# A decoder layer with 39 expert tiles: fewer waits at each tile on TensorE, two barriers replaced by waits, four pieces of work in another order

## What is computed

```python
x = layernorm(x + attention(x, Wq, Wk, Wv, Wo, bo))     # causal, 16 heads of 64
x = layernorm(x + slot_attention(x, ctx, ...))          # 3 iterations with a GRU cell
x = layernorm(ffn(x, ...))

def ffn(x):                                             # 2048 tokens of 256
    values, experts = top_k(softmax(x @ gate_w + gate_b), k=2)
    values = values / (sum(values) + 1e-9)
    out_e  = gelu(x @ ew1[e] + eb1[e]) @ ew2[e] + eb2[e]   # 8 experts, 1024 wide
    return x + gelu(x @ sh_w1 + sh_b1) @ sh_w2 + sh_b2 + sum(values * out_of_the_two_experts)
```

## Time and profile before

| what | us |
|---|---|
| median of 3 runs | 873.48 (873.08 to 873.78) |
| the profiled execution | 875.04 |
| its span, first to last instruction | 873.8 |
| PE busy | 851.6 (97%) |
| DVE, ACT, POOL busy | 605.5, 547.6, 391.0 |

### The profile page before, as it was taken

One profiled execution on the slowest core, in us unless ns is written; L12 is line 12 of the kernel. 1 busy time (PEld: TensorE's weight loads), 2 busy tenths in 40 slices (PEclk: granted clock), 3 DMA queues, 4 the chain that ended last, 5 costly groups with the idle time before them and its releaser, 6 DMA issues. The chain is left out here.

```text
span 873.8 us, 22869 instructions
## 1 busy us (share of the span) xinstructions
PE 851.6 (97%) x8048; PEld 675.1 (77%) x8048; DVE 605.5 (69%) x1638; ACT 547.6 (63%) x1218; POOL 391.0 (45%) x494
## 2 busy tenths in 40 slices
PE   8999999999999999999999999998999999999996
PEld 7788888888888888767676666675788888887864
DVE  5676779775668685656666767888776666666655
ACT  5888887867676776565756565664444444444455
POOL 4544534352433475334544442544635445454443
PEclk9999999999999999999999999999999999999999
DMA  9843424334233321500000000299775555655426
GB/s 312 223 146 127 164 99 146 123 121 146 98 122 122 121 98 49 105 2 1 1 2 1 1 1 1 91 339 300 257 144 74 75 74 75 75 74 74 56 26 199
DMA packets 83627, 93.15 MB, mean 107 GB/s; under 512 B 38559, under 2 KB 69343, under 8 KB 83391
## 3 DMA queue, kind: packets, MB, share of 16 engines
q1 hardware_dynamic: 75487, 80.90, 29.8%
q0 software_dynamic: 7488, 10.27, 10.0%
q10 hardware_dynamic: 544, 0.52, 0.2%
HBM read 56.00 MB, written 30.56 MB: 99 GB/s over the span
## 5 line engine op out<-in xcount | busy, mean ns | idle before, releaser
L663 POOL TENSOR_SCALAR prob<-prob,rden 128x128 f32<-128x128 f32 (+1 forms) x256 | 122.0, 494 | 159.3 <-DVE rden L981 159.3
L2299 PE MATMUL ps<-slots,e 128*128 128x128 f16 x1248 | 126.9, 220 | 0.0
L864 ACT ACTIVATE prob<-prob,nmx 128x128 f32<-128x128 f32 (+1 forms) x256 | 113.2, 446 | 11.3 <-DVE nmx L975 11.3
L2299 PEld LDWEIGHTS ps<-slots,e 128*128 x1248 | 101.4, 97 | 21.9 <-issue 1.1
L2386 ACT ACTIVATE slots<-slots 128x512 f32<-128x512 f32 x78 | 49.1, 630 | 110.4 <-DVE slots L2431 110.4
L2307 PE MATMUL ps<-e,xT 128*128 x312 | 117.3, 378 | 0.0
L2268 POOL DMA_INDIRECT back_y<-xs,dst x39 | 69.0, 1769 | 99.5 <-ACT xs L2398 50.6
L975 DVE CUSTOM_DVE_ANT_0 prob<-ps,mask 128x128 f32<-128x128 f32 (+1 forms) x256 | 73.6, 353 | 34.9 <-PE ps L751 34.9
L31 PE MATMUL ps<-xT,wqkv 128*128 128x256 f16 x768 | 94.7, 273 | 1.8 <-ACT slots L871 1.4
L31 PEld LDWEIGHTS ps<-xT,wqkv 128*128 128x128 f16 x768 | 72.0, 98 | 17.1 <-issue 6.2
L2308 PE MATMUL ps<-e,xT 128*128 x312 | 85.0, 273 | 0.0
(11 more groups left out here) (279 smaller groups left out, 1903.3 us busy)
## 6 DMA issues: line engine op xcount, KB each, us to landing
halves<-parted SPq DMA_DIRECT2D x36, 512.0 KB, 2.9
piece<-in_L_ffn_ew SPq DMA_DIRECT2D x32, 512.0 KB, 4.4
e<-halves SPq DMA_DIRECT2D x16, 1024.0 KB, 11.7
piece<-in_L_ffn_sh_w SPq DMA_DIRECT2D x4, 512.0 KB, 10.3
sw<-halves SPq DMA_DIRECT2D x4, 512.0 KB, 6.5
xs<-back_y SPq DMA_DIRECT2D x8, 256.0 KB, 5.1
out<-xs SPq DMA_DIRECT2D x8, 256.0 KB, 2.9
xs<-in_x SPq DMA_DIRECT2D x1, 1536.0 KB, 12.7
```

The lines of the kernel that those rows point to most:

```text
L663: PO.tensor_scalar(prob[u][:, h, r], prob[u][:, h, r], rden[u][:, h, t:t + 1], 1.0, ALU.mult, ALU.mult).then_inc(normed, 1)
L864: SC.activation(at, at, ACT.Exp, bias=nmx[u][:, h, t:t + 1], scale=-1.0, accum_out=den[u][:, h, t:t + 1]).then_inc(exped, 1)
L2299: yield PE.matmul(ps[:, 2 * u + q, (k % 4) * P:(k % 4) * P + P], w[ch][h], xgT[i % TURNED][:, j * DC + ch, :], start=n == 0, stop=n == 3 * ...
```

## The change

1. The barrier at the start (L491) and the two between attention and slots are gone. In place of the latter two ACT waits, ahead of `rms_out(0)`, for the attention's last sums, the zeroed rows and the last staged pieces; SP waits for the folded weights (`xw_out`) ahead of the loads of the shared weights.
2. The beginning: 8 transposes (not 16) in the second block; `turn_inputs(1)` and `project_v(0)` fill other places; ACT and DVE cut the first weights ahead of the first input; part 6 goes from POOL to ACT.
3. Routing: the first token part's low half is made earlier, the stores go to other places among the loads, `counts` goes behind `up(13)`, and PE reads the experts' numbers between an up and a down.
4. Expert tiles: of the waits of a pair only the turned rows and `U_lo` stay. One pair, ahead of the second reading of the experts' numbers, makes all its ups first and then its downs (`apart`).
5. The end: the sums are loaded in the order 0, 1, 2, 3, 6, 7, 4, 5, and `add_sums` goes just ahead of the last down of the first half.

```diff
-            nc.all_engine_barrier()
...
-            HIGH_BY_POOL = (6, 7)
+            HIGH_BY_POOL = (7,)
...
-            HIGH_AT = {-2: (3, 4), 0: (8, 9), 1: (10,), 2: (11,), 3: (12,)}
+            HIGH_AT = {-2: (4, 5), 0: (8, 9), 1: (10,), 2: (11,), 3: (12,)}
...
                 turn_inputs(0)
-                for n in range(WARM):
+                for n in range(WARM // 2):
...
+                    if j == FIRST:
+                        turn_inputs(1)
+                    if j == -1:
+                        project_v(0)
                     if j + 2 < STAGES:
                         project_qk(2 * (j + 2) + 1)
-                    if j == FIRST:
-                        turn_inputs(1)
...
+                weight_high(SC, 0)
                 inputs_high(0)
-                weight_high(SC, 0)
...
-                        exponentials(0, (1, 2))
+                        exponentials(0, (1,))
+                        weight_high(SC, 6)
+                        exponentials(0, (2,))
...
-            nc.all_engine_barrier()
...
-            nc.all_engine_barrier()
...
                 vw_high(5)
+                SC.wait_ge(y_out, 2 * NB)
+                SC.wait_ge(zeroed, 32)
+                for q in range(PIECES - STAGED, PIECES):
+                    SC.wait_ge(p_out[q % STAGED], 16 * (q // STAGED + 1))
                 rms_out(0)
...
+                SY.wait_ge(xw_out, KEYS + len(FOLDED))
                 for q in range(SHARED_PIECES):
...
-            STORE_AT = {(3, 0): (0, 1), (4, 1): (2,), (5, 0): (3, 4)}
+            STORE_AT = {(3, 0): (0,), (3, 1): (1,), (4, 1): (2, 3, 4)}
...
-                          8: [lambda: norm_gate(2)]}
+                          8: [lambda: norm_gate(2)], 13: [counts]}
...
-                          9: [lambda: norm_forth(3)], 10: [lambda: norm_gate(3)], 12: [counts], 13: [before],
+                          9: [lambda: norm_forth(3)], 10: [lambda: norm_gate(3)], 13: [before],
...
                     if m == 3:
                         norm_scale(2)
                         norm_logits(1)
+                        token_low(0)
...
                         norm_scale(3)
-                        token_low(0)
...
-                def tile_pair(up, e_up, down, e_down):
-
+                def tile_pair(up, e_up, down, e_down, apart=False):
+
+                    if down is not None:
+                        PE.wait_ge(U_lo, down + 1)
                     if up is not None:
                         rows_turned(PE, up)
-                    if down is not None:
-                        PE.wait_ge(U_lo, down + 1)
-                        PE.wait_ge(U_hi, down + 1)
-                        if down >= 2:
-                            PE.wait_ge(D_out, 2 * (down - 1))
...
                     for k in range(IC):
-                        if up is not None and up >= 2 and k % 4 == 0:
-                            PE.wait_ge(U_bias, 2 * (up - 2) + k // 4 + 1)
...
-                            for mm in itertools.islice(downs, 1):
+                            for mm in itertools.islice(downs, 0 if apart else 1):
...
+                    for k in range(IC if apart else 0):
+                        for mm in down_chunk(down, e_down, k):
+                            last_down = mm
...
                         for m in range(MS - 3, MS):
                             if n == 0:
+                                if m == MS - 1:
+                                    add_sums()
...
-                for q in (0, 1, *range(EARLY // CT, CHUNKS), *range(2, EARLY // CT)):
+                for q in (0, 1, 2, 3, *range(EARLY // CT, CHUNKS), *range(4, EARLY // CT)):
```

More of the change, by code:

```diff
@@ L612, in attention_sync @@
                 SY.dma_start(xs[:, 2:4, :], xv[:, 2:4, :]).then_inc(x_in[1], 16)
-                for h, landed in ((1, w_more), (2, w_rest)):
+                for h in (1, 2):
                     for n, k in ((WQ, "q"), (WK, "k"), (WV, "v")):
+                        landed = w_more if h == 1 else w_last if n == WV else w_rest
                         SY.dma_start(into[n][:, :, COLS[h]], wv[k][:, :, COLS[h]]).then_inc(landed, 16)
@@ L646, in weight_high @@
                     engine.wait_ge(w_in[n], 16)
+                elif h == 1:
+                    engine.wait_ge(w_more, 48)
+                elif n == WV:
+                    engine.wait_ge(w_last, 16)
                 else:
-                    engine.wait_ge(w_more if h == 1 else w_rest, 48)
+                    engine.wait_ge(w_rest, 32)
                 hi = weight_part(wqkv[0][:, :, n, :] if n < 3 else wo[0][:, :, :], n, h)
@@ L777, in project_v @@
                     if m == 1:
-                        PE.wait_ge(w_lo, 6)
+                        PE.wait_ge(w_lo, 8)
                     if m == DOUBLES // 2:
@@ L928, in attention_scalar @@
                         prep_scalar(share_at(j), 6)
+                    if j == FIRST:
+                        inputs_high(1)
+                        weight_high(SC, 3)
+                        queries_keys(1)
                     for i in HIGH_AT.get(j, ()):
                         weight_high(SC, i)
-                    if j + 2 < STAGES and j != -1:
+                    if j + 2 < STAGES and j >= 0:
                         queries_keys(2 * (j + 2) + 1)
@@ L1029, in attention_vector @@
                         masks(j + 1, 0)
+                        if j == 0:
+                            reciprocals(0, 1)
                         masks(j + 1, 1)
+                    if j == 0:
+                        weight_low(5)
                     if j == LAST:
@@ L1054, in attention_vector @@
                         folded_low(q)
+                    if j == FIRST:
+                        inputs_low(1)
                     for i in LOW_AT.get(j, ()):
@@ L1992, in ffn_tensor @@
                         up(m)
+                    if m in READ_AT:
+                        PE.wait_ge(r_line, TILES_KNOWN)
+                        first_experts.extend(experts_from(mybir.EngineType.PE, LOADED * READ_AT.index(m)))
                     for work in beside.get(m, ()):
@@ L2369, in experts_tensor @@
                             expert += experts_from(mybir.EngineType.PE, i + 2)
-                        tile_pair(i + 2, expert[i + 2], i, expert[i])
+                        tile_pair(i + 2, expert[i + 2], i, expert[i], i + 3 == len(READ_AT) * LOADED)
                     else:
@@ L2377, in experts_tensor @@
                         down(m - 2)
-                add_sums()
                 last_downs()
```

19 lines of the change are left out of this document (5 added, 14 removed).

## The result

The changed kernel takes 864.34 us (864.1 to 864.43, 4 runs) against 873.57 (873.08 to 873.78, 4 runs): ratio 0.9888, 95% interval 0.9874 to 0.9903. The profiled execution took 864.1 us with a span of 862.9.

What follows compares the result with a forecast made beforehand. PE, busy 851.6 of 873.8 us, was taken as the bound. Terms 0.8 + 0.9 + 2.3 + 3.2 + 0 - 0.4 + 1.0 = 7.8 us took the profiled 875.04 to 867.2, or 865.7 for the median; range 862.6 to 869.6.

Steps and rivals of the forecast that it cites:

- start: Beginning of the kernel: barrier gone, reordering and fewer filler transposes together save 0.8 us (0 to 1.6).
- seam: Between attention and slots: PE no longer stands for the barriers, added waits cost nothing, 0.9 us (0.4 to 1.0).
- routing: Routing stretch: `rows_of(0)` reached sooner through earlier last stores, and the wait at `counts` filled, 2.3 us (0.9 to 2.9).
- tiles: Expert tiles: fewer waits in PE's instruction feed save 0.09 us for each of 36 pairs, 3.2 us (0 to 5.8).
- apart: Pair ahead of the second reading of experts' numbers: ups first, then downs, gives 0 us (-0.4 to +0.4).
- scatters: Behind the expert tiles: scatter chain close to the pairs' pace, slow ones caught up more slowly, -0.4 us (-1.5 to 0).
- end: End of the kernel: parts 2 and 3 of the sums loaded two places earlier, 1.0 us (0.3 to 1.4).
- 5.33 to 5.37 us: Expert tiles: time between tile starts, per pair, that would show the forecast right.
- rival (c): Routing: second store late, `choose_experts` with it, routing gives 0.9, time 867.1; counted within the forecast's chance of 0.63.
- sign of being wrong in routing: Routing: `choose_experts` idle over 1 us for a store would show the routing forecast wrong.
- Rival (d): Start: PE keeps half pace longer, making the kernel slower than before, at about 875.5 us; chance 0.02.

Runs made afterwards that it cites:

- g_old: The changed kernel with the attention part in the order of before, still without the barrier at the start: 867.73 us, ratio to before 0.9914.
- b_again: The kernel before, with no edit, run again for a second profile: 876.22 us, ratio 1.0.

## Why the prediction was right, and where its sizes were off

| step | forecast | the two profiles | undone alone (profile) |
|---|---|---|---|
| start | 0.8 | 1.56 | 1.24 without the barrier |
| seam | 0.9 | 1.12 | 0.8 |
| slots | none | 0.39 | not tried |
| routing | 2.3 | 1.5 | 0.16 |
| tiles, `apart`, scatters | 2.8 | 4.9 | 4.8 (waits), 0.06 (`apart`) |
| end | 1.0 | 1.4 | 0.6, within the spread |
| sum | 7.8 | 10.9 | |

The total came close in part by luck: routing fell short of its term and the tiles went beyond theirs. The runs with one step undone bear out the tiles, the seam and the start. All steps undone alone, with the barrier's 0.32 us at the start, make 7 to 8 us, so for part of the gain no run shows what it comes from.

**Tiles.** The mechanism is as forecast: PE is fed too slowly there, and what stands in the feed at a boundary is paid. The size was not. The prediction had the price of one feed instruction, 0.13 us, and the bound of 0.16, and took 0.09. Measured: 0.14 a pair (5.44 to 5.30) for one wait instruction and the middle condition less, none for a condition in a wait instruction that stays. So pairs were shorter than the 5.33 to 5.37 us that the prediction gave as its sign. The Trainium skill ("TensorE: Matmul & The Clock Gate", "Step-by-step: what each phase is for") says that the sequencer takes the next instruction as soon as one is committed; the prediction drew from it that a condition long met would be hidden. That came out wrong for the pairs and right behind `apart`: there even the old waits cost nothing for two pairs (5.28 us each), and with the new ones the pace of 5.28 lasts for the six pairs up to 822.87.

**Scatters.** The term of -0.4 did not appear. 23 of 39 now wait for a landing in place of 17, but the last is issued 9.5 us earlier (840.80 for 850.30), as far ahead as PE. A late landing can still reach the end, as in the run with the old beginning.

**Routing.** The step that failed is the second store. The prediction let it be up to 0.6 us late, and 0.9 for the whole stretch if it was over 1 us late. `choose_experts` waited 3.04 us for it, so it was rival (c), and the prediction's own sign of being wrong in routing, over 1 us of idle for a store, came. The last stores did come before `part_choices(0)` needed them, so that wait is gone, but PE's wait at `rows_of(0)` is not: it went from 2.37 to 1.80 us, since DVE starts the first part late and takes 3.0 us for it (597.14 to 600.15). The stretch gained 1.5 of the 2.3, and with the edits undone it lost only 0.16, so little of that gain is shown to be theirs. A second price of such a wait, which the sum did not have, is the fall of the granted clock in the second profile of before.

**Start.** Of the waits that were counted at 1.7 us, of which 0.5 was taken, 0.9 is left (0.25 and 0.66), so 0.8 went. The filler was worth more than the prediction allowed: eight transposes take 1.61 us where sixteen took 1.95, and 2.36 in `g_old`, which is as slow there as the first profile of the change; against that run most of the 1.24 is filler (0.75) and the rest waits. The barrier gave 0.32, as taken. **Seam**: right. **End**: the wait of 1.86 fell to 0.19 as forecast, but parts 4 and 5 now keep DVE waiting 0.51 us, which the term left out, and what is left over is not clear of the spread. **Rival (d)**, half pace at the start for longer, did not occur: the first projection takes 1.47 us in both profiles.

## What to carry to other kernels

Where every few matmuls need an address from a register, PE's instruction feed is the bound, and the view of waits shows nothing of it: compare the pace with and without the address instructions, and count wait instructions first, not conditions. Waits that come from one chain (DVE's low half behind ACT's high half) need one wait on the last link. A wait of 2.3 us on TensorE cost 1.6 us of clock behind it in one profile and nothing in another of the same kernel, so it can be worth more than its length, and one profile may not show it. And a stretch that is shorter in the profile after is not yet the work of its edits: the routing stretch kept most of its gain with the edits undone.

## What the runs showed of the hardware

The pace of TensorE changes during the first transposes at a moment that differs between executions: eight of them took 1.61 us in the first profile of the change and 1.04 in the second, where PE then waited 0.75 us for the input's low part, so that 0.47 us remained of it at the first projection. The view's granted clock reads 1.00 for both.

The kernel before spread over 874.4 to 878.4 us in 13 runs on one chip. All seven with a mean granted clock of 0.995 or 0.996 took 875.86 us or more, all six at 0.998 took 875.67 or less. The ten runs of `b_again`, the same kernel on the same chip, keep less to this: three at 0.998 took 875.99 to 876.23, and the longest, 878.90, had 0.997. So the clock goes with part of the spread only. The page of the Trainium skill named above gives the two levels in "What's actually happening" as 1.2 and 2.4 GHz; a down of 2.77 us at a granted 0.50 against 1.47 at 1.00 agrees.
